# Splitting the first token chain in two groups, and moving V of unit 0, in a fused attention and expert kernel on one Trainium2 core

## What is computed

```python
def _L0_xattn_ref(latents, tokens, ...):      # latents 8x56x128, tokens (the context) 8x1500x128
    q = _ln(latents, sa_ln_g, sa_ln_b)
    x = latents + _mha(q, q, ...)             # self-attention, 16 heads of 8
    qc = _ln(x, ca_q_ln_g, ca_q_ln_b)
    kv = _ln(tokens, ca_kv_ln_g, ca_kv_ln_b)
    x = x + _mha(qc, kv, ...)                 # cross-attention over 1500 context rows
    return _fuse_moe(x, ...)                  # layer norm, top 2 of 8 experts, gelu
def _L1_xattn_ref(x, context, ...):
    xn = layer_norm(x, ln_gamma, ln_beta)
    q = xn @ bit_quant(Wq).T + bq
    k = context @ bit_quant(Wk).T + bk
    v = context @ bit_quant(Wv).T + bv
    probs = jax.nn.softmax(scores, axis=-1)
    return residual + (out @ bit_quant(Wo).T + bo)
```

## Time and profile before

| | us |
|---|---|
| median of 3 runs | 576.63 |
| lowest and highest | 573.84, 576.68 |
| the profiled execution, its own time | 574.07 |
| its span, first to last instruction | 572.3 |
| PE busy in the span | 514.1 (90%) |
| DVE busy | 390.0 (68%) |
| ACT busy | 334.4 (58%) |
| POOL busy | 221.3 (39%) |

### The profile page before, as it was taken

One profiled execution on the slowest core, in us unless ns is written; L12 is line 12 of the kernel. 1 busy time (PEld: TensorE's weight loads), 2 busy tenths in 40 slices (PEclk: granted clock), 3 DMA queues, 4 the chain that ended last, 5 costly groups with the idle time before them and its releaser, 6 DMA issues.

```text
span 572.3 us, 16262 instructions
## 1 busy us (share of the span) xinstructions
PE 514.1 (90%) x6648; PEld 386.4 (68%) x6648; DVE 390.0 (68%) x976; ACT 334.4 (58%) x527; POOL 221.3 (39%) x217
## 2 busy tenths in 40 slices
PE   3599748889999999999989999999998999999996
PEld 2588515466767767676767998877666676766774
DVE  5666378788887888787741434887867777786730
ACT  1166223557676777776576444376666667675573
POOL 3659744475777768423160200031404033140000
PEclk9799677899999999999999999999999999999998
DMA  5110552634354554555638401006354835535200
GB/s 160 48 55 3 143 122 50 169 89 132 95 139 112 143 145 101 137 120 143 182 73 223 141 2 31 2 1 154 72 150 113 201 92 140 144 85 121 56 4 9
DMA packets 37869, 58.69 MB, mean 103 GB/s; under 512 B 17956, under 2 KB 21404, under 8 KB 37796
## 3 DMA queue, kind: packets, MB, share of 16 engines
q1 hardware_dynamic: 37476, 57.60, 39.8%
q10 hardware_dynamic: 320, 0.06, 0.1%
HBM read 17.81 MB, written 0.23 MB: 32 GB/s over the span
## 4 chain that ended last, share of the span: by engine, by line
PE 68%; DVE 17%; POOL 4%; DMA 3%; issue 3%; ACT 2%; SPq 2%; DVEq 0%; ACTq 0%; POOLq 0%
PE PO L1386 14%; PE SM L1371 14%; DVE mxp L883 11%; PE ST L1343 10%; PE MI L1292 8%; PE ST L1564 4%; PE ST L1554 4%; PE MI L1282 3%; PE MI L1271 2%; POOL cxs L518 2%; PE MI L1318 2%; DMA xT<-in_ctxT 1%; ACT pts L671 1%; PE SM L1477 1%; SPq L393 1%
## 5 line engine op out<-in xcount | busy, mean ns | idle before, releaser
L883 DVE TENSOR_REDUCE mxp<-SM 112x1 f32<-112x500 f32 x374 | 241.0, 673 | 74.4 <-PE SM L1371 73.2
L671 ACT ACTIVATE pts<-ST 128x896 f32<-128x896 f32 x192 | 171.7, 913 | 31.3 <-PE ST L1343 30.8
L1371 PE MATMUL SM<-kst,qst 96*112 96x500 bf16 x374 | 142.2, 399 | 13.0 <-DVE mxp L883 9.0
L527 POOL TENSOR_TENSOR kr<-kf,ksplit 128x500 f32<-128x500 f32 x48 | 55.1, 1150 | 172.4 <-ACT ksplit L636 172.4
L1343 PEld LDWEIGHTS ST<-qst,kst 98*128 98x128 bf16 x1536 | 95.8, 100 | 29.5 <-issue 4.7
L1343 PE MATMUL ST<-qst,kst 98*128 98x112 bf16 x1536 | 106.9, 213 | 2.6 <-DMA qst<-mrow 2.6
L1386 PE MATMUL PO<-pts,vaug 125*32 125x112 f32 x3072 | 97.3, 263 | 2.3 <-ACT pts L671 1.9
L1371 PEld LDWEIGHTS SM<-kst,qst 96*112 96x112 bf16 x374 | 45.6, 129 | 61.5 <-DVE mxp L883 45.0
L1386 PEld LDWEIGHTS PO<-pts,vaug 125*32 125x32 f32 x3072 | 69.3, 109 | 14.8 <-ACT pts L671 5.7
L518 POOL TENSOR_SCALAR cxs<-cxs,cmv,crstd 125x128 f32<-125x128 f32 x84 | 67.4, 819 | 0.0
L532 POOL TENSOR_TENSOR ksplit<-kr,ksplit 128x500 bf16<-128x500 f32 x48 | 54.4, 1135 | 16.9 <-DVE ksplit L878 16.9
(11 more groups left out here) (156 smaller groups left out, 539.8 us busy)
## 6 DMA issues: line engine op xcount, KB each, us to landing
kst<-ksplit SPq DMA_DIRECT2D x192, 187.5 KB, 3.6
cxs<-in_ctx SPq DMA_DIRECT2D x8, 750.0 KB
xT<-in_ctxT SPq DMA_DIRECT2D x8, 750.0 KB, 6.5
qst<-qall SPq DMA_DIRECT2D x56, 21.0 KB, 1.9
watt<-in_watt SPq DMA_DIRECT2D x1, 768.0 KB, 5.5
cxs<-in_w1T SPq DMA_DIRECT2D x3, 256.0 KB, 5.7
cxs<-in_w2T SPq DMA_DIRECT2D x3, 256.0 KB, 6.3
pts<-in_w1T SPq DMA_DIRECT2D x3, 256.0 KB, 5.4
```

What stands on the lines that cost most here:

```text
L527: nc.gpsimd.tensor_tensor(kr[:, c], kf[:, c], ksplit[n.par][:, 0, c], ALU.subtract).then_inc(kr_done, 1)
L671: nc.scalar.activation(PT[:, k % PTB], ST[:, k % 2, :, 0:4 * PC], ACT.Exp, scale=SCALE).then_inc(exp_done, 1)
L883: nc.vector.tensor_reduce(mxp[:, j // 3, j % 3:j % 3 + 1], tile_bank(j, banks), AX.X, ALU.max).then_inc(sm_red, 1)
L1371: mm(tile_bank(j, banks), qst[n.par][0:SROWS, j // 3], kst[n.par][0:SROWS, j // 3, at:at + THIRD], start=True, stop=True).then_inc(sm_full, 1)
```

## The change

**The first chain runs in two groups.** `PARTS` names the token tiles of each projection; group 0 is token tile 0, group 1 the tiles 1 to 3. Group 0's links are put one to a step of self-attention: the projection (`"out"`) on PE in step 6, add and statistics on DVE in step 7, normalisation in 8 with the transpose (`"ln"`) on PE, the gain in 9 with the query projection (`"q"`), the split in 10. V of unit 0 stands in steps 10 and 11 (`"v"`). The copies to `qall` are one group at a time; units 0 and 1 need group 0 alone.

**Group 1's links stand between the start tiles**, of which there are now 21: projection and add at tile 2, normalisation at 7, gain at 9, query projection at 12, split at 14 to 16. Window 0 has three tiles less. Half of the context statistics of unit 3 stand at tile 12, the other half and their aggregation in window 0; its root moves there on POOL.

**On SP** the context load of unit 3 is moved from ahead of unit 0's stacks to behind `load_qall(0)`, and the new `load_qall(1)` stands behind the first half stack of unit 1. **In the second layer** the links of the second half of the tokens are moved: statistics from step 9 of window 0 to step 4, normalisation from 11 to 9, transpose from step 3 of window 1 to step 10 of window 0, query projection from step 9 to 10 of window 1, the splits one step later each.

```diff
-START_TILES = 18
+START_TILES = 21
-FIRST_TILES = spread_tiles(TILES - START_TILES, (3, 3, 3, 3, 2, 2, 3, 3, 2, 2, 2, 2))
+FIRST_TILES = spread_tiles(TILES - START_TILES, (3, 3, 3, 3, 2, 2, 2, 2, 2, 2, 2, 1))
-LN5_AT, Q2_AT = (1, 3), (1, 9)
-SPLIT2_AT = ((1, 10), (1, 11), (2, 0))
+LN5_AT, Q2_AT = (0, 10), (1, 10)
+START_OUT, START_ADD, START_NORM, START_LN, START_Q, START_SPLIT = 2, 3, 7, 9, 13, (14, 15, 16)
+SPLIT2_AT = ((1, 11), (2, 0), (2, 1))
-             5: (("k", 0, 2),), 7: (("t", 1, 0),), 8: (("t", 1, 1),), 9: (("t", 1, 2),)}
+             5: (("k", 0, 2),), 6: (("-", 0, 0), ("out", 0, 0)), 7: (("t", 1, 0),), 8: (("t", 1, 1), ("ln", 0, 0)),
+             9: (("t", 1, 2), ("q", 0, 0)), 10: (("-", 0, 0), ("v", 0, 0)), 11: (("v", 0, 1), ("v", 0, 2))}
+PARTS = (range(0, 1), range(1, TT), range(0, HT), range(HT, TT), range(0, HT), range(HT, TT))
...
             load_ctx(Unit(0, None, 2))
-            load_ctx(Unit(0, None, 3))
             restack(u0, 0)
             restack(u0, 1)
             load_qall(0)
+            load_ctx(Unit(0, None, 3))
             place(u1, 0)
             restack(u1, 0)
+            load_qall(1)
...
@@ POOL
+                if i == 7:
+                    token_rstd(1)
-            token_rstd(1)
+            k_parts(u1, None, lambda: token_rstd(2))
             ctx_normalise(u0 + 2, (2,))
-            k_parts(u1, None)
-            ctx_rstd(u0 + 3)
@@ DVE
-            add_projection(0)
-            token_stats(1)
-            token_normalise(1)
-            ctx_stats(u0 + 3, range(5))
-            token_gain(1)
-            split_q(0)
-            ctx_stats(u0 + 3, range(5, NCH))
...
             place_q(first, 0)
+            place_q(first, 1)
             for j in range(START_TILES):
                 reduce_tile(first, j, banks=4)
-                if j == 3:
-                    place_q(first, 1)
-                if j in (1, 4, 7):
-                    k_second_part(first + 1, j // 3)
+                if j == START_ADD:
+                    add_projection(1)
+                    token_stats(2)
+                if j == START_NORM:
+                    token_normalise(2)
+                if j == START_LN:
+                    token_gain(2)
+                if j in START_SPLIT:
+                    split_q(1, (START_SPLIT.index(j),))
+                if j in (1, 5, 12):
+                    k_second_part(first + 1, (1, 5, 12).index(j))
                 if j == TILES // 2 - 1:
                     max_parts(first, 0)
+                if j == TILES // 2:
+                    ctx_stats(u0 + 3, range(6))
@@ PE
-            pe.wait_ge(ld_rows, 48)
-            project_out(0, (sa_att, B))
             prev = project_k_apart(u1, prev)
-            transpose_tokens(1)
-            project_q(0, 1)
             for j in range(START_TILES):
                 max_tile(u0, j, banks=4)
-                if j in (1, 4, 7):
-                    prev = project_v(u0, j // 3, prev)
-                if j in (10, 13, 16):
-                    prev = transpose_ctx(u0 + 2, (10, 13, 16).index(j), prev)
+                if j == START_OUT:
+                    project_out(1, (sa_att, B))
+                if j == START_LN - 1:
+                    prev = transpose_tokens(2, prev)
+                if j == START_Q - 1:
+                    prev = project_q(1, prev)
+                if j in (10, 14, 17):
+                    prev = transpose_ctx(u0 + 2, (10, 14, 17).index(j), prev)
```

More of the change, by code:

```diff
@@ L710, in start_pass @@
                 first = Unit(0, None, 0)
-                for i in range(3):
-                    evac_v(first, i)
                 evac_xT(first + 2, (0, 1))
@@ L729, in evac_piece @@
                     evac_xT(n, (third,))
-                else:
+                if kind == "k":
                     evac_k(n, third)
+                if kind == "v":
+                    evac_v(n, third)
             for i in range(SA_STEPS):
@@ L1228, in project_out @@
                 pe.wait_ge(*done)
-                layer = (n + 1) // 2
-                ts = range(TT) if n == 0 else range(HT * ((n - 1) % 2), HT * ((n - 1) % 2 + 1))
-                bank = MI if n in (1, 3) else PO
-                for i, t in enumerate(ts):
+                layer = n // 2
+                bank = PO if n % 2 else MI
+                for i, t in enumerate(PARTS[n]):
                     tile = bank[0:TP, D * i:D * (i + 1)]
```

162 lines of the change are left out of this document (95 added, 67 removed).

## The result

| | before | after |
|---|---|---|
| median of 4 runs, us | 576.05 | 583.68 |
| lowest and highest | 573.84, 576.68 | 583.22, 584.60 |
| profiled execution, its own time | 574.07 | 583.27 |
| its span | 572.3 | 581.4 |

A forecast was written before the change was run, and what follows sets the result against it. Up to the first start tile a PE chain of latency was taken as the bound, behind it DVE's work. First layer -0.4 and second layer -1.2 sum to -1.6 us: 575.0 from the median 576.63, range 571.0 to 579.5.

The forecast's parts named there:

- part 1: End of self-attention to the first start tile: group 0's shorter chain opens that tile at 79.1, 7.0 us earlier.
- part 2: Start tiles with group 1's chain on DVE: scores at about 102.5, tile 21 at 103.1, 2.3 us won.
- part 3: Window 0, tile 21 to window 1: moved work adds 1.9 us, between 0.6 and 2.3; first part of kernel nets -0.4.
- New ahead of it, in steps 6 and 7: Self-attention, ahead of the stacks: group 0's projection, add, statistics and root delay their start by 0 to +0.8 us.
- Rival 4: Self-attention step 7: POOL's new root holds the last third part 3 to 4 us, stacks start late; 578.5 us, chance 0.07.
- Wrong would be: Signs against the forecast: first tile waiting for PE's own keys, a context-load wait in window 0, or changed other windows.
- rival 1: Start tiles: PE's clock falls just as the projection begins, +2.2 us, 577.2 us; chance 0.22.
- unit 3's root behind its parts: Window 0 on POOL: unit 3's root moved behind its parts, transposed at step 9, claimed to cost nothing.
- Part 4: Second layer: waits at transpose, V projection and query projection leave with the new places; -1.2 us, between 0 and -2.
- Costed at nothing: Moves given no time: V of unit 0, unit 3's context and root, a third of unit 2's normalisation.
- Rival 3: SP in window 0: more copies make unit 4's context load late, so later tiles wait; 581 us on the median, chance 0.07.

The follow-up runs named there:

- e3: Changed kernel, late add kept, with six matmuls nobody reads on PE in step 7 where it waits for MI; 581.06 us, ratio 1.0066 to before.
- e2: Changed kernel with group 0's add moved from step 7 to step 6 on DVE, ahead of the context statistics; 577.94 us, ratio 1.0029 to before.
- e11: e10 with the cast move of e5 and idle matmuls as in e6 (10, 4 and 4); 576.32 us, ratio 0.9938 to before.
- e6: e2 with matmuls nobody reads in PE's waits ahead of the first tile and behind tiles 6, 7 and 14; 575.60 us, ratio 0.9955 to before.
- e5: e2 with unit 1's second cast on DVE moved from behind tile 5 to behind tile 2; 579.42 us, ratio 1.0020 to before.
- e1: Kernel before with only the second layer's moves of the change; 572.80 us, ratio 0.9926 to before.
- e0: Kernel before, unchanged, profiled once more for a second trace; its own time 584.19 us.
- e10: e2 with V of unit 0 moved from self-attention's last steps to behind start tiles 3, 5 and 6; 579.43 us, ratio 1.0015 to before.
- e7: e1 plus V of unit 0 in self-attention's steps 10 and 11, the chain in one group; 578.66 us, ratio 0.9982 to before.
- e8: e1 plus 12 matmuls nobody reads in PE's wait ahead of the first start tile; 572.84 us, ratio 0.9916 to before.

## Why the prediction was wrong, point by point

From step 5 to window 1 the forecast had 88.1 us and after took 98.8. Of these 10.7 us, 6.2 arose ahead of the first tile (part 1), 2.7 between it and the scores (part 2) and 1.8 in window 0 (part 3).

**Part 1 failed in one clause.** "New ahead of it, in steps 6 and 7 ... I count 0 to +0.8." I counted the durations of the new DVE work and left out who waits for it. The add frees MI, and PE's next context transpose needs MI; the add stood behind 3.8 us of other DVE work. The step measured +3.4 us at the stacks (24.0 against 20.7), of which the clock made 2.0 (e3). I had listed the waits of PE in steps 8 to 11 and not the one in step 7. Rival 4 named this place, but as POOL's root holding the third part, and gave it 0.07; the root was ready in time. "Wrong would be: the first tile waiting for PE's own keys" is what happened. With the add in its place (e2) the first tile was at 37.1 from step 5, 80.05 in its own trace: the rest of part 1 was right within 1 us.

**Part 2.** The sum was met once, by e11 (23.6 for 23.4), in part by luck: its normalisation took 1.90 where I had 1.2, its casts 0.41 each without the 0.8 that I had added. The kernel as it stood did not meet its sizes: 26.1 in after, 27.5 in e2. In e2 the clock cost 2.2 (rival 1, which I had at 0.22): two of the projection's three tiles ran at half clock, and e6 took that away. My argument against that rival, that a longer idle stretch was needed, did not hold: in e2 the clock fell behind a wait of 3.18 us, and in before itself it reads 0.90 from 60 to 62, where PE was busy for 1.42 us of the two. The cast took 2.33, 1.9 more than its 0.40, where I had 0.8 more and at most 1.4: it met POOL's two-input operations as in the 56.61 row, and I should have taken that row and not a value between.

The normalisation took 0.84 in after, which is less than the 1.2 that I had, but POOL was at work for only the first 0.1 us of it. Beside POOL's rest and third part it took 2.57 (e5) and 1.90 (e11). The Trainium skill, SBUF — State Buffer, section Who interferes with whom, says that VectorE in a two-port mode and GpSimd lock each other out for a whole instruction, and counts cast and `tensor_scalar`, the normalisation's operation, among those that can enter such a mode. The traces agree for both where they met two of POOL's two-input operations in a row. They do not where the cast met POOL's TENSOR_SCALAR: 0.40 us at 54.02 in after.

**The saving itself was mis-weighed.** Before, 15.6 us of tiles follow the first tile; with group 1's chain among them they need 23.4 at best. I had both numbers, so of 7 us won I expected to lose almost 8 and kept 2.3 by counting three more tiles. That held (e11). But the whole yield then hung on the small difference of two large terms, and any one mis-sized item decided its sign. The chance of a measurably slower kernel should have been far over 0.12.

**Part 3 came near, in part by luck.** From tile 21 to the scores of window 1 I had 27.3, and at most 27.7. In after it took 28.8, from 113.48 to 142.24, with the clock at 0.50 up to 116; in e2, where it was 1.00 throughout, 27.5. Both hold PE's wait of 1.55 us for POOL ahead of window 1. I had costed "unit 3's root behind its parts" at nothing; the last step ahead of window 1 took 1.3 us more for it. That leaves some 0.8 in e2 for the work that I had counted at 1.9.

**Part 4 had the right sign and a third of the size.** Forecast -1.2, between 0 and -2; measured -3.7 over the second layer's first windows in the traces and -4.3 in e1's runs (-2.3 to -6.3). The term was mis-sized: all three waits left with the new places (0.52, 0.80 and 0.63 in before, 1.9 us together), but with them went the stop on issue in window 2 (1.68 in before, 1.86 in e0), which I had not looked for, since I had read windows 1 and 3 alone.

**Costed at nothing, V of unit 0:** wrong as a habit. In the split kernel moving it back gained nothing (e10), with the chain in one group it cost 2.9 us at the first tile (e7). **Rival 3** did not show: unit 4's context load was issued at 119.9 in after, later than I had it, and no wait of window 0 names it.

The difference of 10.3 us at window 1 divides, but for rounding, into 5.5 for the late add (after to e2), 3.7 for what e11 took out of e2, all of it ahead of the scores, and 1.2 for e11 against before, of which some 0.7 are the wait for POOL.

## What to carry to other kernels

When a result goes through a shared buffer, the cost of a new link is not its own 0.28 us but how long the next user of the buffer stands behind it: place the reader ahead of the long work of its engine, and look at the buffer's next user in the other engine's list. A step that hides a chain beside other work is worth only what the other work leaves free; compare the stretch before with the same stretch after, both whole, ahead of counting what opens earlier. A wait on TensorE can cost more than its length: this one put the stacks 1.7 us late by itself and 2.0 more by the clock behind it. And an operation that is moved out of another engine's way may leave the next one in it, as the cast of e5 did: read the rows of both engines again after the move.

## What was not expected of the hardware

One wait of 2.99 us on PE was followed by the lower clock until the stretch of 86 to 88; the same place with idle matmuls in it kept 1.00 until 64. Idle matmuls in one gap (e8) gained nothing that can be told, and the clock was down longer behind the next wait; in several gaps (e6) they gained 2 to 4 us. The same cast took 0.40 us beside POOL's TENSOR_SCALAR, 2.33 to 2.43 where it began just behind the start of two TENSOR_TENSOR in a row, and 0.41 in the midst of a single one (after, 120.50), which then took 1.84 instead of 1.13; a normalisation of three tiles took 0.84 without such a pair and 1.90 and 2.57 with it. A stop of 1.7 to 1.9 us on instruction issue stood at the same matmul in three traces of two kernels (439.25, 442.34 and 449.13) and in none with the second layer's moves; what makes it is open. And the moment at which the clock rises again in self-attention put the same instruction at 42.9 and at 46.1 in two executions of one kernel, and at 42.7 to 50.6 over all kernels here, whose programs are alike up to it, so two profiles can be compared only from a common mark behind it.
